# A two-layer attention and FFN kernel: VectorE's and ScalarE's order within the first attention

## What is computed

```python
x = x + L0_xattn(layernorm(x), ctx)   # 16 heads of 16; 48 main keys and 16 extra keys (dca), two softmaxes, added
x = x + L0_ffn(layernorm(x))          # 256 -> 768 -> 256, weights rounded to e4m3, silu(gate) * up
x = x + L1_xattn(layernorm(x), ctx)   # 16 heads of 128, RMS-normed queries and keys
x = x + L1_ffn(layernorm(x))          # 256 -> 1024 -> 256, in e4m3 and bf16
```

```python
q = ln(x @ Wq + bq) * qn_w + qn_b;  k = ln(y @ Wk + bk) * kn_w + kn_b   # mean and variance over the head's 16
p = softmax(q k^T / 4)  over the main keys, and another over the dca keys
x = x + (p_main v_main + p_dca v_dca) @ Wo + bo
```

## Time and profile before

| what | us |
|---|---|
| three runs | 766.05, 766.55, 763.95; median 766.05 |
| the profiled execution | 761.46 |
| its span | 759.7 |
| busy in the span | PE 663.7, DVE 567.5, ACT 486.7, POOL 440.4 |
| DMA, mean share of the 16 engines, 60 to 165 us | 0.11 |

### The profile page before, as it was taken

The page is one execution under the profiler, slowest core; times in us unless marked ns, Lnnn a source line. Parts: engine busy times, 40 slices in busy tenths (PEclk is TensorE's granted clock), DMA queues, the critical chain, the costliest instruction groups (busy, mean ns, idle before and its releaser), DMA issues.

```text
span 759.7 us, 16367 instructions
## 1 busy us (share of the span) xinstructions
PE 663.7 (87%) x5782; PEld 529.8 (70%) x5782; DVE 567.5 (75%) x1282; ACT 486.7 (64%) x996; POOL 440.4 (58%) x648
## 2 busy tenths in 40 slices
PE   1688888876999999999999999999999999877773
PEld 1566666655888877888888888888888888754331
DVE  3599999997588877767676676677676766738996
ACT  1367666664566667666666666666666666657894
POOL 2477787877777734655656666665565644443200
PEclk9999999998999999999999999999999999999997
DMA  9200000500410000000010100100000000000001
GB/s 273 67 6 9 8 9 9 171 1 1 125 57 28 8 15 1 16 22 15 15 29 9 35 13 18 29 8 22 23 15 23 1 1 2 2 1 1 28 28 56
DMA packets 26019, 22.83 MB, mean 30 GB/s; under 512 B 5041, under 2 KB 24402, under 8 KB 25810
## 3 DMA queue, kind: packets, MB, share of 16 engines
q1 hardware_dynamic: 24688, 21.44, 9.1%
q10 hardware_dynamic: 1250, 0.33, 0.2%
HBM read 19.67 MB, written 2.10 MB: 29 GB/s over the span
## 4 chain that ended last, share of the span: by engine, by line
PE 60%; DVE 20%; issue 10%; ACT 6%; POOL 2%; DMA 1%; SPq 0%; DVEq 0%; ACTq 0%; POOLq 0%
PE banks L1559 12%; PE banks L1269 7%; PE banks L1271 6%; PE banks L1270 6%; PE banks L1638 4%; PE banks L1612 4%; PE banks L1604 4%; PE banks L1568 4%; PE banks L1415 3%; PE banks L1436 3%; PE banks L1437 3%; ACT prob L1082 2%; DVE h_sum L1005 2%; DVE hid L1008 2%; PE banks L1590 1%
## 5 line engine op out<-in xcount | busy, mean ns | idle before, releaser
L681 POOL TENSOR_TENSOR rstd<-var,minus_half 128x8 f32<-128x8 f32 x65 | 107.7, 1657 | 5.1
L672 POOL TENSOR_TENSOR p_n<-pr,pinv 128x256 f32<-128x256 f32 x64 | 39.3, 613 | 79.7 <-DVE pinv L916 79.7
L657 POOL TENSOR_TENSOR pr<-pr,rstd 128x256 f32<-128x256 f32 x64 | 39.2, 613 | 78.8 <-DVE pr L955 78.8
L1559 PE MATMUL banks<-m_hi,z_hi 128*128 128x256 f32 x256 | 74.5, 291 | 7.5 <-DVE z_lo L908 7.4
L1194 ACT ACTIVATE kT<-banks,gk_q 128x512 f32<-128x512 f32 x64 | 44.1, 690 | 50.6 <-PE banks L1568 50.6
L1559 PE MATMUL banks<-m_hi,z_lo 128*128 128x256 f32 x256 | 72.1, 282 | 0.0
L1559 PE MATMUL banks<-m_lo,z_hi 128*128 128x256 f32 x256 | 72.1, 282 | 0.0
L908 DVE TENSOR_TENSOR z_lo<-banks,z_hi 128x512 fp32r<-128x512 f32 x64 | 43.9, 686 | 31.2 <-ACT z_hi L1160 31.2
L935 DVE TENSOR_REDUCE sums<-q_sq 128x4 f32<-128x512 f32 x64 | 43.7, 683 | 25.8 <-ACT q_sq L1175 25.8
L951 DVE TENSOR_REDUCE pmax<-banks 128x4 f32<-128x256 f32 x64 | 27.0, 422 | 46.3 <-PE banks L1604 46.3
L1559 PEld LDWEIGHTS banks<-m_hi,z_hi 128*128 128x128 f32 x256 | 48.3, 189 | 17.4 <-DVE z_lo L908 15.9
(11 more groups left out here) (189 smaller groups left out, 2087.3 us busy)
## 6 DMA issues: line engine op xcount, KB each, us to landing
w_raw<-in_L_xattn_Wq SPq DMA_DIRECT2D x4, 512.0 KB, 6.4
wo_raw<-in_L_xattn_Wo SPq DMA_DIRECT2D x1, 2048.0 KB, 8.3
k_ctx<-in_ctx SPq DMA_DIRECT2D x16, 128.0 KB, 2.7
w_raw<-in_L_ffn_w_gating SPq DMA_DIRECT2D x16, 128.0 KB, 2.3
out_x<-x_sb SPq DMA_DIRECT2D x4, 512.0 KB, 3.0
x_sb<-in_x SPq DMA_DIRECT2D x1, 1536.0 KB, 8.9
a_ctx<-in_ctx SPq DMA_DIRECT2D x16, 64.0 KB, 1.8
w_raw<-in_L_xattn_Wk SPq DMA_DIRECT2D x2, 512.0 KB, 9.5
```

The lines of the kernel that those rows point to most:

```text
L672: pool.tensor_tensor(p_n[:, 1 - par, :, :], pr[:, 1 - par, :, :], pinv[:, 1 - par, :].unsqueeze(2).to_broadcast([P, HC, S]), ALU.mult).the ...
L681: pool.tensor_tensor(rstd1[:, par, :], var1[:, :], minus_half[:, :].to_broadcast([P, 2 * HC]), ALU.pow).then_inc(root1, 1)
L1559: last = nc.tensor.matmul(bank[6][:, za * D:(za + 1) * D], z[:, odd, c, :], mm[:, h, :], start=w % NS == 0 and c == 0 and m == 0, stop=w % ...
```

## The change

On VectorE the constants for the weight chunk move from the end of the step to directly behind the guess of the roots. The centring of tile i+2 moves ahead of the bias and of the sums. On ScalarE the square moves ahead of the main-key copies. Nothing is added or removed.

```diff
@@ vector, step(i, k)
                     first_guess(dve, LN_N * t + 1, half2[:, t % 2, :, 0], qk_mean[:, :], rstd2[:, t % 2, :, 0], qk_tmp[:, t % 2, :])
+                for c in chunks(i):
+                    if c == 0:
+                        dve.wait_ge(w0_in, 3 * 16)
+                    after(dve, w0_steps, 2 * (c - 1))
+                    e4m3_magic(dve, magic_steps, 2 * c, w0_raw[:, c * W_CHUNK:(c + 1) * W_CHUNK], rnd2[:, c % 2, :, 0])
                 t = i
 ...
                     moments(dve, 1, t, 1)
+                t = i + 2
+                if live(t, NT):
+                    dve.wait_ge(qk_done, t + 1)
+                    after(dve, scaled, t - 1)
+                    after(dve, sq_ready, t - 1)
+                    dve.tensor_tensor(qk_cent[:, t % 2, :, :]..., bank[1][:, :], bqk[:, :, :]..., ALU.add).then_inc(cent_ready, 1)
                 if i == 0:
                     dve.wait_ge(bo_done, 1)
 ...
                     dve.tensor_reduce(ssum[:, 1, :], prob[:, t % 2, :, MAIN:S], AX.X, ALU.add).then_inc(sum_ready, 1)
-                t = i + 2
-                if live(t, NT):
-                    ... (the centring, as above)
-                t = i
-                if live(t, NT):
                     dve.wait_ge(sum_ready, 2 * t + 2)
                     after(dve, prob_ready, 2 * (t - 1))
                     dve.reciprocal(sinv[:, t % 2, :, :], ssum[:, :, :]).then_inc(inv_ready, 1)
-                for c in chunks(i):
-                    ... (the constants, as above)
@@ scalar, step(i, k)
                                    scale=cols[:, 0, 0:1], bias=cols[:, 0, 1:2]).then_inc(t_evac, 1)
-                    turned_keys(t, 0)
                 t = i + 2
                 if live(t, NT):
                     act.wait_ge(cent_ready, t + 1)
 ...
                     act.activation(qk_sq[:, :, :], qk_cent[:, t % 2, :, :], ACT.Square).then_inc(sq_ready, 1)
                 t = i + 1
                 if live(t, NT):
+                    turned_keys(t, 0)
                     turned_keys(t, 1)
```

More of the change, by code:

```diff
@@ L778, in step @@
                     moments(dve, 1, t, 1)
+                t = i + 2
[3 more added lines that the diff above has]
+                    after(dve, sq_ready, t - 1)
+                    dve.tensor_tensor(qk_cent[:, t % 2, :, :].rearrange("p h d -> p (h d)"), bank[1][:, :],
+                                      bqk[:, :, :].rearrange("p s n -> p (s n)"), ALU.add).then_inc(cent_ready, 1)
                 if i == 0:
```

## The result

| | before | changed |
|---|---|---|
| median of 22 runs each, us | 765.17 (762.55 to 769.12) | 762.37 (759.67 to 765.01) |
| ratio | | 0.9959, 95% interval 0.9946 to 0.9972 |
| first profiled execution, us (span) | 761.46 (759.7) | 759.77 (758.0) |
| tile 4's sum of squares (L754) starts at | 63.14 | 59.03 |
| tile 15's | 167.72 | 161.73 |

A forecast was written before the change was run, and what follows sets the result against it. VectorE's queue was taken to bound the steady tiles; -4.4 (first tiles), -2.1 (eleven steady tiles) and +4.6 (last tiles) gave -1.9 us, so 764.2 us from a median of 766.05; own range 761.5 to 766.5, with rivals 756.5 to 768.

The forecast's parts named there:

- The hold: Steady tiles: L406 and L408 on VectorE wait for the ends of GpSimd's two scaling instructions (L624), costing 1.19 us a tile.
- The first rival: Steady tiles: small single-input VectorE steps (L406, L408, L410) are not held by GpSimd's scaling; 758 us, chance 0.15.
- the one in which L408 slips in: Rival, steady tiles: L408 runs before the scaling's second half, saving 0.22 us a tile; 761.8 us, chance 0.18.
- The pair: Steady tiles: the two rounding constants L427 and L429, behind the guess, cost 0.49 us in place of 1.80, 1.31 saved.
- The slow rival: Steady tiles: L427 and L429 each wait for a Newton operation of GpSimd; 9.7 us a tile, 768.5 us, chance 0.17.
- The centring: Steady tiles: centring ahead of the sums removes the 0.19 us exponentials wait, but the reciprocal follows serially; net 0.07 saved.
- Period: Time of one steady tile on VectorE: 9.31 us against 9.50, 0.19 saved a tile, 2.1 us over 11 tiles.
- ScalarE's order: Square ahead of the key copies costs nothing; with the copies ahead VectorE would wait 0.3 us at L754.
- The start: First tiles, where VectorE waits: 4.4 us gained, bounds 2.5 and 5.5.
- The end: Last tiles: 4.6 us given back, 3.8 of it from tile 15's maxima waiting behind chunk 16's constants; bounds 1.5 and 5.5.
- The sum: Start, steady tiles and end together: 1.9 us gained at the FFN's start, carried over to the median as 764.2 us.

The follow-up runs named there:

- The short scaling: The changed kernel with GpSimd scaling only the first key of each of the two parts, the other scaling left out: 747.09 us, ratio 0.9766.

## Why the prediction was right, and what was off

**The hold.** Right in place and size. L406 was to end at about the first half's end and L408 at the second's, L416 to start 3.26 after the reciprocal: 99.43 less 96.20 is 3.23. The short scaling took the hold away. The Trainium skill names the contention for VectorE instructions in a 2-port mode or with two inputs in SBUF ("GPSIMD Engine Reference", 1. Specifications); the traces agree for L406, a step of 32 columns with a single input that the prediction counted among them (1.01 us in place of 0.18). The first rival (small steps pass, 758 us) is refuted, and so is the one in which L408 slips in.

**The pair.** 0.49 forecast; from L427's start to L770's it is 0.53. The slow rival, Newton's operations ahead of the pair, did not occur: L396 started at 99.70 while L427 was running, and L429 still took 0.30.

**The centring.** The wait for the exponentials is gone and the reciprocal follows the sums serially, as forecast. By the two halves alone, the constants give 0.12 of the 0.18 us a tile and the centring nothing without them. Period: 9.31 forecast, 9.32 read, 1.9 us over eleven tiles in place of 2.1.

**ScalarE's order.** That it costs nothing was right. That without it VectorE would wait 0.3 was near (0.18), but the step implied that this wait would lengthen the tile, and that was wrong: a wait ahead of a held instruction is taken out of the hold.

**The start.** 4.4 forecast, 4.1 read in the first pair of traces, though with other clocks. In the changed kernel the centring and the bias, moved ahead, waited 0.77 and 0.39 us for TensorE, which had part of that stretch at the lower clock (0.95 is the mean of 28 to 60 us):

```profile
36.44 0.69 DVE L791 TENSOR_TENSOR qk_cent<-banks,bqk 128x512 f32<-128x512 f32 x1 [0.77 <-PE banks L1315]
...
37.52 0.42 DVE L796 TENSOR_TENSOR bo_bc<-banks,bo_bc 128x256 f32<-128x256 f32 x1 [0.39 <-PE banks L1325]
```

**The end.** 13.85 forecast for tile 15's maxima after L754, 13.81 read; given back 4.6 forecast, 4.4 read (28.3 against 23.8 us). Behind the maxima 0.6 of it was read (14.4 against 13.8) where 0.8 was forecast. One term was off and did not show: the scores were to be ready at 11.2 and ended at 13.1 (12.5 and 12.8 in the other two traces), with TensorE at its lower level from 166.7 to 173.9 us and waits of its own. Chunk 16 came later still, by 0.7, so the maxima stood where they were forecast.

**The sum.** -4.4 - 2.1 + 4.6 = -1.9 forecast; -4.1 - 1.9 + 4.4 = -1.6 at the FFN, -1.7 in the profiled executions. The medians say -2.8. The term at fault is the last step, "the same difference gives 764.2": it took the one trace of before as the typical one, and the end's +4.6 as a constant. In that trace the scores of the last tile were ready as early as they are in any of the three; with the clock lower there, before loses up to 2.4 us more up to its maxima, and the maxima of the changed kernel do not move, so the loss is 4.4 us against one trace and 2.0 against another (28.3 less 26.3). By the means over the traces above the FFN starts at 193.6 before and at 189.9 with the change, 3.7 us apart: 5.2 gained up to tile 4, 2.2 in the eleven tiles, 3.7 given back. So against the first pair half of the surplus lies in the first tiles, where the later traces of before came later (63.82 and 65.40 at tile 4, after 63.14), and a third in the last ones. Of the 3.7 the means behind the FFN's start take back 1.4 us (568.6 against 570.0), which with 3 and 4 traces can't be told from chance. So the sign and the place of the surplus are shown, its exact size is not.

**Where this left the ranges.** Faster was given 0.45 and within 0.3% 0.42; the changed kernel is 0.41% faster, just past the line between the two, on the side of faster; the forecast itself, 0.25%, was on the other side. 762.4 lies inside the forecast's own range of 761.5 to 766.5. No rival brought it there: the measured time lies near the 761.8 of the one in which L408 slips in, and the trace refutes that one.

## What to carry to other kernels

Before moving an instruction on VectorE, look at what GpSimd runs at the new place: a held instruction here cost the rest of GpSimd's instruction whatever its own size (1.01 us for one of 0.18), so put there what is not held, or what has to wait anyway. Walk the first and last steps of a software pipeline by themselves; here the end gave back 4.4 us, more than eleven steady tiles gained (1.9), and moving its last two chunks returned 1.5 us, or 3.2 where the scores were early. And take the waits for TensorE from several traces: a schedule that waits for it moves with its clock, one that waits for something else does not.

## What the hardware showed beside this

The hold alternates. VectorE gets one held instruction through at the end of each GpSimd instruction, and GpSimd's next one, if it is queued, runs before VectorE's next: from tile 5 of the changed kernel on, L406 ends with the first half and L408 with the second. Not every instruction of GpSimd holds: its multiplications and additions of 256 columns and more do (L624, L618), its power on 128x4 (1.03 and 1.07 us) does not. Whether that is the operation or its four columns, no run here separates. In the first tiles of the changed kernel L446 starts at 41.89, lasts 1.07 us, and L410 runs inside it at its usual length:

```profile
42.10 0.18 DVE L410 TENSOR_SCALAR rstd<-rstd 128x32 uint32<-128x32 uint32 x1
```

It is not that VectorE's step is small: with ScalarE's order undone, L427, of 256 columns, starts at 108.55 inside an L446 (107.93 to 108.96) and takes 0.29 us.

On VectorE's side the sums (L754), the reciprocal and the centring from PSUM, which has one of its two inputs there, kept 0.63 to 0.69, 0.35 and 0.63 us beside GpSimd instructions of 0.73 and 2.05 us.
